# The last batch of the first attention in an order of its own

## What is computed

```python
x = x + L0_xattn(layernorm(x), ctx, ctx)      # this layer, its last batch
#   q, k, v = heads of query @ w_q.T + b_q, key @ w_k.T + b_k, value @ w_v.T + b_v
#   attn = softmax(q k^T / 4);  out = (attn v) @ w_o.T + b_o
x = x + L0_attn(layernorm(x))                 # a filter along the batch axis, then silu
x = x + L0_ffn(layernorm(x))                  # 16 experts, 4 chosen
x = x + L1_xattn(...); x = x + L1_attn(...); x = x + L1_ffn(...)
```

## Time and profile before

| | us |
|---|---|
| median of 3 runs | 746.31 |
| lowest and highest of the 3 | 743.70, 746.61 |
| span of the profiled execution | 743.2 |
| TensorE busy in it | 692.6 |
| VectorE busy | 536.9 |
| GpSimd busy | 434.9 |
| ScalarE busy | 414.0 |
| mean granted clock of TensorE | 0.982 |

### The profile page before, as it was taken

One profiled execution on the slowest core, in us unless ns is written; L12 is line 12 of the kernel. 1 busy time (PEld: TensorE's weight loads), 2 busy tenths in 40 slices (PEclk: granted clock), 3 DMA queues, 4 the chain that ended last, 5 costly groups with the idle time before them and its releaser, 6 DMA issues.

```text
span 743.2 us, 15612 instructions
## 1 busy us (share of the span) xinstructions
PE 692.6 (93%) x5750; PEld 568.0 (76%) x5750; DVE 536.9 (72%) x1189; ACT 414.0 (56%) x788; POOL 434.9 (59%) x457
## 2 busy tenths in 40 slices
PE   5799999999999797999999999999998889999987
PEld 2577877777777686999999999996455456666776
DVE  5678878777788646337777777754646899997576
ACT  3556656666655423366666666651327986665532
POOL 4638634646446123867778777746216698896120
PEclk9999999999999886999999999999999999999999
DMA  8201101101002339899989999985864700001000
GB/s 339 108 4 59 58 1 56 36 21 57 0 13 101 114 161 404 300 392 376 400 342 335 331 332 343 350 322 182 338 257 150 286 1 1 1 0 44 1 1 28
DMA packets 20476, 123.50 MB, mean 166 GB/s; under 512 B 2288, under 2 KB 6784, under 8 KB 13120
## 3 DMA queue, kind: packets, MB, share of 16 engines
q1 hardware_dynamic: 17488, 114.72, 40.6%
q0 software_dynamic: 2928, 8.00, 3.0%
HBM read 111.90 MB, written 10.81 MB: 165 GB/s over the span
## 4 chain that ended last, share of the span: by engine, by line
PE 74%; DVE 11%; ACT 7%; POOL 3%; issue 2%; DMA 1%; SPq 0%; DVEq 0%; ACTq 0%; PEldq 0%; POOLq 0%
PE banks L2136 64%; PE banks L2205 8%; POOL inject L1000 2%; DVE shown L1997 2%; DMA ctx_raw<-in_ctxT 1%; ACT probs L1081 1%; DVE banks L2006 1%; DVE negmax_raw L1568 1%; ACT banks L1340 1%; PE banks L2373 1%; PE banks L2667 1%; DVE shown L2018 1%; ACT ctx_hi L1067 1%; DVE X L2095 1%; ACT turned_back L1351 0%
## 5 line engine op out<-in xcount | busy, mean ns | idle before, releaser
L2136 PE MATMUL banks<-xT,raw 128*128 128x128 f32 x992 | 152.0, 276 | 0.6 <-DVE xT L1783 0.6
L2136 PEld LDWEIGHTS banks<-xT,raw 128*128 128x128 f32 x992 | 135.3, 193 | 3.1 <-issue 1.2
L931 POOL TENSOR_TENSOR w_lo<-raw,w_hi 128x1024 fp32r<-128x1024 f32 x50 | 118.0, 2384 | 1.8 <-ACT w_hi L1174 1.0
L1205 ACT ACTIVATE banks<-banks,later 128x128 f32<-128x128 f32 x200 | 67.9, 340 | 56.3 <-PE banks L2136 54.8
L1110 ACT ACTIVATE probsT<-banks 128x512 f32<-128x512 f32 x64 | 38.3, 598 | 85.3 <-PE banks L2205 85.0
L1000 POOL TENSOR_TENSOR inject<-BCbc,drive 128x1024 f32<-128x1024 f32 x32 | 75.1, 2360 | 13.8 <-DVE shown L1997 8.5
L1789 DVE CAST mid_hi<-banks 128x128 fp32r<-128x128 f32 x200 | 57.8, 289 | 33.6 <-ACT banks L1205 31.9
L1568 DVE TENSOR_REDUCE negmax_raw<-banks 128x1 f32<-128x1024 f32 x64 | 77.6, 1212 | 2.9 <-PE banks L2136 2.9
L1081 ACT ACTIVATE probs<-banks,negmax 128x1024 f32<-128x1024 f32 x64 | 71.2, 1112 | 10.9 <-DVE negmax L1570 10.8
L2205 PE MATMUL banks<-table,probs 128*128 128x128 f32 x512 | 71.1, 283 | 2.1 <-DVE probsT L1541 2.1
L2136 PE MATMUL banks<-w_hi,mid_hi 128*128 128x256 f32 x200 | 72.5, 362 | 0.0
(11 more groups left out here) (348 smaller groups left out, 1741.9 us busy)
## 6 DMA issues: line engine op xcount, KB each, us to landing
raw<-in_w SPq DMA_DIRECT2D x31, 2048.0 KB, 9.1
ctx_raw<-in_ctxT SPq DMA_DIRECT2D x8, 1024.0 KB, 4.9
ctxT<-in_ctxT SPq DMA_DIRECT2D x4, 2048.0 KB, 8.8
ctxN<-in_ctxN SPq DMA_DIRECT2D x4, 2048.0 KB, 13.9
x_slots<-zero SPq DMA_DIRECT2D x1, 3968.0 KB, 12.0
y_slots<-y_tile POOLq DMA_DIRECT2D x29, 128.0 KB, 7.0
wf<-in_w SPq DMA_DIRECT2D x9, 384.0 KB, 5.5
BCbc<-bc_rows SPq DMA_DIRECT2D x6, 512.0 KB, 7.0
```

The costliest lines, as they stand in the source:

```text
L931: nc.gpsimd.tensor_tensor(w2_lo[i % WB][:, cols], raw[i % WB][:, EW // 2:][:, cols], w2_hi[i % 2][:, cols].bitcast(F32), ALU.subtract).the ...
L1205: nc.scalar.activation(to, held, ACT.Gelu, bias=b1[:, bass.ds(at + u, 1)]).then_inc(gelu_done, 1)
L2136: return nc.tensor.matmul(o, lhsT, rhs, start=start, stop=stop)
```

## The change

Three of the engines get a `last_batch` of their own in place of `batch(B - 1, ...)` and what followed it. On VectorE the two maxima of a duo now follow each other, then come the value piece and one copy of a turned half. ScalarE copies both halves of the pairs 0, 2, 4 and 6 and the second half of the others; VectorE keeps the first half of 1, 3, 5 and 7. Values 3 are projected in duo 2 rather than 3. The three remaining quarters of the weighting of batch 6 stand together in duo 1, and the batch's own first four quarters stand between the turns of duo 3. Turn 6 goes to banks 0 and 1 (`LAST_TURN_BANKS`), the last weighting to bank 4 (`LAST_SPREAD_BANK`), the tokens for the filter to banks 2 and 3; the filter's two banks change places. The norm statistics of tiles 0 to 2 come behind the last maxima, tiles 0 and 1 are normalised before the last two gathers and tile 2 after them. GpSimd makes the inverse diagonals of the last batch between the first powers of the norm. The last output projection is split: its first half stands before the transposes of the tokens, its second after them. In the other batches only the arguments change. Context lines and hunks that carry only such arguments are left out.

```diff
@@ -84,7 +84,8 @@
...
-FRONT_BANKS, REST_BANK, BACK_BANKS = (4, 5), 6, (2, 3, 0)
+FRONT_BANKS, REST_BANK, BACK_BANKS = (5, 4), 6, (2, 3, 0)
+TURN_BANKS, LAST_TURN_BANKS, SPREAD_BANK, LAST_SPREAD_BANK, EARLY_TURN_BANKS = (5, 6), (0, 1), 7, 4, (2, 3)
...
@@ -442,6 +443,7 @@
...
+        sixth_ready, conv_before = conv_ready, 2
...
@@ -895,11 +897,11 @@
...
-            for t in range(TC - 1):
+            diagonals(B - 1, 0)
+            rstd_of(2, 0)
+            diagonals(B - 1, 1)
+            for t in range(1, TC):
...
-            diagonals(B - 1, 0)
-            diagonals(B - 1, 1)
-            rstd_of(2, TC - 1)
...
@@ -1100,15 +1102,37 @@
...
-                    if not (last and later_b):
-                        key_piece(key_at(b, d), c, half)
+                    key_piece(key_at(b, d), c, half)
+
+            def turned_half1(b, i, half, bank, ready):
+
+                c, j = divmod(i, PAIRS)
+                act.wait_ge(t_done, 16 * b + 2 * i + 1 + half)
+                nc.scalar.activation(probsT[c][:, half * KC // 2:(half + 1) * KC // 2, j, :], pb(bank).rearrange("p (k n) -> p k n", n=P),
+                                     ACT.Copy).then_inc(ready, 1)
...
-
-                c, j = divmod(i, PAIRS)
-                act.wait_ge(t_done, 16 * b + 2 * i + 2)
-                nc.scalar.activation(probsT[c][:, KC // 2:KC, j, :], pb(6).rearrange("p (k n) -> p k n", n=P),
-                                     ACT.Copy).then_inc(pt1_ready, 1)
+                turned_half1(b, i, 1, TURN_BANKS[1], pt1_ready)
+
+            def both_halves(b, i):
+                turned_half1(b, i, 0, TURN_BANKS[0], pt0_ready)
+                second_half(b, i)
+
+            def last_batch(b):
+                second_half(b - 1, 6)
+                weights1(b, 0)
+                second_half(b - 1, 7)
+                weights1(b, 1)
+                _, c, half = KEY_TURN[0]
+                key_piece(key_at(b, 0), c, half)
+                for d in range(1, DUOS):
+                    both_halves(b, 2 * d - 2)
+                    weights1(b, 2 * d)
+                    weights1(b, 2 * d + 1)
+                    second_half(b, 2 * d - 1)
+                for half in range(2):
+                    turned_half1(b, 6, half, LAST_TURN_BANKS[half], sixth_ready)
+                second_half(b, 7)
...
@@ -1129,23 +1153,22 @@
...
-                batch(b, b % 2, b == B - 1)
-            second_half(B - 1, 6)
-            second_half(B - 1, 7)
+                batch(b, b % 2)
+            last_batch(B - 1)
-                nc.scalar.activation(xnT[:, c, 0:FRONT], pb(c)[:, 0:FRONT], ACT.Copy).then_inc(front_ready, 1)
+                nc.scalar.activation(xnT[:, c, 0:FRONT], pb(EARLY_TURN_BANKS[c])[:, 0:FRONT], ACT.Copy).then_inc(front_ready, 1)
...
@@ -1569,16 +1592,8 @@
...
-            def batch(b, par, last, tile=None):
+            def batch(b, par, tile=None):
...
-
-                def norm_ahead(i):
-                    if last and 1 <= i < TC:
-                        dve.wait_ge(tile_added, i + 1)
-                        norm_begin(2, i - 1)
-                    if last and 5 <= i < TC + 4:
-                        norm_tile(2, i - 5)
-
...
@@ -1591,37 +1606,71 @@
...
-                    value_piece(value_at(b, d, last), par, d)
-                    norm_ahead(2 * d)
+                    value_piece(value_at(b, d), par, d)
...
-                    norm_ahead(2 * d + 1)
...
-                    if not (last and later_b):
-                        key_piece(4 * b + (len(FIRST_BANKS) + d + 1), c, half)
+                    key_piece(4 * b + (len(FIRST_BANKS) + d + 1), c, half)
+
+            def last_batch(b, par):
+                invert_sums(b - 1, 1)
+                largest1(b, 0)
+                first_half(b - 1, 6)
+                value_piece(value_at(b, 0, True), par, 0)
+                largest1(b, 1)
+                first_half(b - 1, 7)
+                gather(b - 1, 1 - par, 0)
+                _, c, half = KEY_TURN[0]
+                key_piece(4 * b + len(FIRST_BANKS) + 1, c, half)
+
+                largest1(b, 2)
+                largest1(b, 3)
+                value_piece(value_at(b, 1, True), par, 1)
+                first_half(b, 1)
+                invert_sums(b, 0)
+                gather(b - 1, 1 - par, 1)
+
+                largest1(b, 4)
+                largest1(b, 5)
+                value_piece(value_at(b, 2, True), par, 2)
+                first_half(b, 3)
+                value_piece(value_at(b, 3, True), par, 3)
+
+                largest1(b, 6)
+                largest1(b, 7)
+                first_half(b, 5)
+                norm_ahead(0)
+                invert_sums(b, 1)
+                norm_ahead(1)
+                first_half(b, 7)
+                norm_ahead(2)
+                norm_tile(2, 0)
+                norm_tile(2, 1)
+                gather(b, par, 0)
+                gather(b, par, 1, LAST_SPREAD_BANK)
+                norm_tile(2, 2)
+
+            def norm_ahead(t):
+                dve.wait_ge(tile_added, t + 2)
+                norm_begin(2, t)
...
-            batch(0, 0, False)
+            batch(0, 0)
...
-                batch(2 * n + 1, 1, False)
-                batch(2 * n + 2, 0, False, n)
-            batch(B - 1, 1, True)
-            invert_sums(B - 1, 1)
-            gather(B - 1, 1, 0)
-            first_half(B - 1, 6)
-            first_half(B - 1, 7)
-            gather(B - 1, 1, 1)
+                batch(2 * n + 1, 1)
+                batch(2 * n + 2, 0, n)
+            last_batch(B - 1, 1)
...
@@ -2194,46 +2243,53 @@
...
-            def turn(b, i):
+            def turn(b, i, banks=TURN_BANKS, before=None):
...
-                    if not (isinstance(b, int) and b == 0 and i == 0):
-                        pe.wait_ge(pt1_ready if half else pt0_ready, 8 * b + i)
+                    if banks is TURN_BANKS and not (isinstance(b, int) and b == 0 and i == 0):
+                        pe.wait_ge(pt1_ready if half else pt0_ready, 8 * b + i if before is None else before)
...
-                        last = nc.tensor.transpose(pb(5 + half)[:, k * P:(k + 1) * P],
+                        last = nc.tensor.transpose(pb(banks[half])[:, k * P:(k + 1) * P],
...
-
-
-                pe.wait_ge(piece_taken, value_at(b, q, isinstance(b, int) and b == B - 1))
+                last_one = isinstance(b, int) and b == B - 1
+                ends = last_one and c == DC - 1
+                bank = pb(LAST_SPREAD_BANK if ends else SPREAD_BANK)
+                pe.wait_ge(piece_taken, value_at(b, 3 if ends else q, last_one))
...
-                    pe.wait_ge(pt0_ready, 8 * b + PAIRS * (c + 1))
-                    pe.wait_ge(pt1_ready, 8 * b + PAIRS * (c + 1))
+                    turned = 8 * b + PAIRS * (c + 1) - (1 if ends else 0)
+                    pe.wait_ge(pt0_ready, turned)
+                    pe.wait_ge(pt1_ready, turned)
...
-                    if not (isinstance(b, int) and b == 0 and c == 0):
+                    if ends:
+                        pe.wait_ge(sixth_ready, 2)
+                    elif not (isinstance(b, int) and b == 0 and c == 0):
...
-                        mm(pb(7)[PAIR_W * j:PAIR_W * (j + 1), P:2 * P], part(table, TABLE, "pick"), inv_diag[:, j, :], True, True)
+                        mm(bank[PAIR_W * j:PAIR_W * (j + 1), P:2 * P], part(table, TABLE, "pick"), inv_diag[:, j, :], True, True)
...
-                        last = mm(pb(7)[PAIR_W * j:PAIR_W * (j + 1), 0:P], V[par][:, kc, at:at + PAIR_W],
+                        last = mm(bank[PAIR_W * j:PAIR_W * (j + 1), 0:P], V[par][:, kc, at:at + PAIR_W],
...
+                for c in range(DC):
+                    last = project_out_part(c)
+                last.then_inc(out_done, 1)
+
+            def project_out_part(c):
...
-                for c in range(DC):
-                    last = mm(pb(7)[:, 256:512], attn[:, c, :], wo[:, c, :], c == 0, c == DC - 1)
-                last.then_inc(out_done, 1)
+                return mm(pb(SPREAD_BANK)[:, 256:512], attn[:, c, :], wo[:, c, :], c == 0, c == DC - 1)
...
@@ -2282,25 +2335,56 @@
...
-                    if not (last and later_b):
-                        project_keys(key_at(b, d), b + later_b, (par + later_b) % 2, c, half)
+                    project_keys(key_at(b, d), b + later_b, (par + later_b) % 2, c, half)
...
+
+            def last_batch(b, par):
+                scores(b, 0)
+                turn(b - 1, 6)
+                project_values(value_at(b, 0, True), par, 0)
+                weigh(b - 1, 1 - par, 0, 2)
+                turn(b - 1, 7)
+                _, c, half = KEY_TURN[0]
+                project_keys(key_at(b, 0), b, par, c, half)
+                weigh(b - 1, 1 - par, 0, 3)
+
+                scores(b, 1)
+                turn(b, 0)
+                project_values(value_at(b, 1, True), par, 1)
+                weigh(b - 1, 1 - par, 1, 0)
+                turn(b, 1)
+                for q in range(1, 4):
```

(53 more changed lines are left out.)

16 lines of the change are left out of this document (8 added, 8 removed).

## The result

The changed kernel takes 734.75 us (median of 4 runs, 734.45 to 735.01), the kernel before 746.46 (4 runs, 743.70 to 746.66). The ratio is 0.9887 with an interval of [0.9853, 0.9922]. As the experiments show, more than half of the size of this one comparison did not come again on other chips.

What follows compares the result with a forecast made beforehand. TensorE was taken as the bound, losing 6.0 us to waits and 4.7 to half clock. A filter 7.9 us earlier cut the span from 743.2 to 735.3; 3.1 from span to median gave 738.4, range 735.8 to 743.0.

Steps and rivals of the forecast that it cites:

- The ledger of the batch: TensorE's path through the last batch rebuilt in the new order: last weighting ends 8.7 us earlier, filter starts 7.9 earlier.
- the norm work: Norm statistics, some 0.75 us a tile, move from between the maxima to where VectorE waits for turn 7.
- the 4.7 for the low clock: Last batch: TensorE's two half-clock stretches cost 4.7 us, which the new order was to win back.
- the one from the span to the time: Whole kernel: the old median lies 3.1 us above the profiled span of 743.2; this was added to 735.3.
- the phase behind the filter: After the filter: a shift of the low clock alone is worth 1 to 2 us in either direction.
- the low clock at the end of the batch: Rival: last turn and weighting run at half clock, costing 2.2 to 3.4 us, time 740.6 to 741.8; chance 0.30.
- slower: Rival: waits around the last weighting drop the clock through filter and turning back, 4.3 us slower, 750.6; chance 0.06.
- The third case: Rival: the stage behind the filter, or late ScalarE and VectorE handovers, takes back 4 to 8 us; chance 0.12.

Runs made afterwards that it cites:

- the copies between the maxima: Changed kernel with VectorE copying all first halves, each even one between the two maxima of its duo; filter 0.58 us later, span 736.5.
- behind them: Changed kernel with VectorE copying all first halves, even ones after both maxima and the value addition; filter 4.19 us later, ratio 1.0014 to the kernel before.
- the turn bank: Changed kernel with turn 6 back in banks 5 and 6; filter 0.95 us later, time 751.79 us.
- the weighting bank: Changed kernel with the last weighting back in bank 7 and the output projection whole behind the transposes; filter 1.49 us later, time 753.95 us.
- the filled kernel: Kernel before the change with five unread matmuls in TensorE's waits of the last batch; median 741.87 against 742.11 us unfilled, ratio 1.0008.
- norm statistics early: Changed kernel with the norm statistics of tiles 0 to 2 back in their old places; 738.17 us against 742.11 for the kernel before, ratio 0.9949.

## Why the prediction was right, and where not

The ledger of the batch held. Scores 2 and 3 at 238.98 and 245.00 (forecast 239.0 and 245.1), last weighting at 253.43 (253.51), filter at 258.37 (258.8). One term makes up most of the 0.4: the last weighting takes 2.10 (253.43 to 255.53), not 2.41, since my 0.54 for a quarter was half of the duration of two, while from start to start a quarter takes 0.47. The weighting also starts 0.08 earlier, and norm tile 2 begins 0.21 after the last sum does (256.31, 256.52), where I had 0.3. Its parts were right one by one: the norm work is worth nothing (0.16), the copies between the maxima 0.58 (0.6 forecast), behind them 4.19 (three times 1.2 to 1.5), the turn bank 0.95 (1.1), the weighting bank 1.49 (1.5).

The term that was mis-sized is the 4.7 for the low clock. As a price of that stretch it is nearly right: 4.1 by the filled kernel. But I put it down as a gain in the time of every run, because one profile showed it. In the three other comparisons the gain was 4.8, 2.8 and (norm statistics early) 3.9 us, where the ledger has 7.9, and at equal clock it is 4.3 to 4.9: the 4.3 of the order alone. Whether the kernel before often runs at full clock there, or the changed kernel pays the low clock behind the filter instead, stays open.

The second step that failed is the one from the span to the time. I set 743.2 beside the three runs and carried the 3.1 to their median. Each run with a span on record lies 1.8 above it (734.72 with 732.9), so the profile of before belongs to a run of about 745.0, which is none of those listed. With 1.8 the ledger would have said 737.1.

The third is the phase behind the filter, which I gave 1 to 2 us either way: it was 1.9 for the change, at the upper end. The low stretch there is 10.1 us long in the changed kernel's first profile and 13.6 before (282.28 to 295.92), so the dispatch and the first expert ran faster; in its later profiles, from about 273 to 290, it is 17 us long. So the 3.7 below the forecast are 0.4 of the ledger, 1.3 of the step from span to time and 1.9 behind the filter. And that this one comparison came as near as that to a ledger with all of the 4.7 in it is luck, since in the others most of it was missing.

Rivals: the low clock at the end of the batch came in none of the profiles, though turns and narrow weighting with no projection between them ran from 245.90 to 255.53. Those are 9.6 us, where the prediction says 8. The Trainium skill (TensorE: Matmul & The Clock Gate, Part 4: PE-mode transpose) states that a transpose does not count as busy in the same way as other matmuls; the fall that the prediction drew from it did not come here (clock 1.00 over this stretch in every profile), and how transposes count no run shows. Nothing was slower. The third case, with 742.5 to 746.5 as its time, did not come in the result; a gain of 2.8 to 4.8, as on the other chips, is near the size it describes (7.9 less 4 or more).

## What to carry to other kernels

Write the critical engine's path out in the new order, from starts to next starts of the old trace, and wait wherever another engine is later: over 26 us and five engines this was right to 0.4. Moving one engine's long operations together pays only if what they push back is moved to another engine or bank in the same change, so price the parts in pairs. And where the profile shows the clock low, price it apart, and count it as gain only when many runs of both kernels show it. Sorting runs by mean clock shows what an order is worth, but hides what a change does through the clock, so give the medians beside it.

## What the runs showed of the hardware

The spread of one unchanged kernel on one chip is 7.8 us of span (737.0 to 744.8), and it falls in step with TensorE's mean granted clock, 0.990 to 0.979. Five matmuls that nothing reads, put into waits, delayed nothing (scores 2 after 7.69 us instead of 7.70); the clock was full for the 38 us around them in the one profile, but the times of the runs did not show it. Five in the router behind the filter went with a full clock there in three profiles of three, against none of eleven without, and that stretch was 1.4 to 3.2 us shorter. Chips differ as well: the same kernel had a median of 742.11 on one and 753.29 and 754.18 on two others.
